# Two attention layers of a graph network: GpSimd's gather program without a loop and without copied indices

## The chip, the cores and the metric

The kernel runs on one core of a Trainium2 chip. A core has five engines that run their own instruction streams side by side and meet at semaphores: TensorE (PE in the profile), VectorE (DVE), ScalarE (ACT), GpSimd (POOL) and SyncE (SP), and 16 DMA engines that move data between the on-chip memory (SBUF) and the chip's main memory. The metric is the device time of one execution in microseconds (us), the median of several runs.

## The reference

Four graph operators stand one behind the other, each followed by a layer normalisation, over 6250 nodes with 64 features and 200000 edges sorted by destination. The change touches the first only, the two attention layers:

```python
def _gat_conv(x, src, dst, W, al, ar, b, act):
    z = (x @ W).reshape(N, H, F)                 # N = 6250, H = 4, F = 64
    el = jnp.sum(z * al, axis=-1)
    er = jnp.sum(z * ar, axis=-1)
    e = jax.nn.leaky_relu(el[src] + er[dst], 0.2)
    m = jax.ops.segment_max(e, dst, num_segments=N)
    ex = jnp.exp(e - m[dst])
    s = jax.ops.segment_sum(ex, dst, num_segments=N)
    alpha = ex / s[dst]
    msg = z[src] * alpha[..., None]
    out = jax.ops.segment_sum(msg, dst, num_segments=N) + b
    return act(out)
...
h = _gat_conv(x, src, dst, W1, al1, ar1, b1, jnp.tanh).mean(axis=-2)
h = _gat_conv(h, src, dst, W2, al2, ar2, b2, lambda v: v).mean(axis=-2)
```

After them come three graph convolutions with edge weights, one plain sum over neighbours and two convolutions with edge features.

## The kernel before

The kernel keeps a table of 6250 rows in main memory (`table_d`: 64 features, a one and four logit parts of each node, 69 floats). In each attention layer the row of every edge's source node is fetched from it. GpSimd does this: `blocks_pool` goes through 98 blocks (`NBLK`) of 2048 edges, each in 16 indirect DMAs (`BK`) of 128 rows, line 826, into one of three ring slots in SBUF (`ring`, `RING` = 3). `gathered[i]` counts what has landed in slot i. Two gathers into the next block stands the store of the finished block to `msg_d` in main memory (`store`, line 800), which waits for all 16 gathers of that block; at the eighth gather GpSimd waits for the store's landing and raises `msg_ready` (`ready`, line 804).

The indices of a gather are a column of `row_idx`. In the loop the block's number is a register, and the gather reads its column not from there but from `idx_cur`, into which a copy on GpSimd (`copy_indices`, line 808) brings four columns at a time (`IDX` = 4), two gathers ahead of their use (`AHEAD_IDX`); the first gather of each four waits for the copy's semaphore `idx_here`. Layer 0's first three blocks are written out, then a loop takes three blocks per turn; layer 1 has its first three blocks written out and then the same loop; the last two blocks of each layer stand behind it. Inside the loop the values that are waited for are computed in registers, and every such wait (`wait_reg`, lines 359 and 360) raises a counter `passed_pool` that nobody reads.

GpSimd is also paced: before every second gather of a block it waits until VectorE's step counter `dve_step` has reached a number that was worked out from the edges (`pace_row`, read into a register on line 812), so that it does not run further ahead of VectorE than intended.

SyncE (`win_sync`) loads for each group of 50 nodes the records (line 505) and, as soon as the block that the group needs is counted in `msg_ready` and the buffer is free, its five windows of messages (`rows_sl<-msg_d`, line 535). VectorE (`win_vector`) does per group: one-hot matrices of edges on adjacency windows (`one_hots`, lines 1051 and 1052; three windows per group in layer 0, two in layer 1), then logits of the messages (`logits`, from line 1074 on, the first instruction that needs them), their maxima (`tops`) and differences. ScalarE and TensorE follow it. There are 125 groups per layer, in 25 rounds of five; a round of VectorE is one turn of its loop. After both attention layers SyncE streams the stored adjacency blocks to TensorE for the six convolutions; GpSimd has nothing to do there. A layer's gathers start from `table_stored`, the landing of its table.

Of the kernel before, what the change touches and what calls it, by code (L numbers as in the profile page):

```python
# [14 lines left out]
I32 = mybir.dt.int32  # L15
# [12 lines left out]
P = 128  # L28
# [55 lines left out]
def build(nc, a):  # L84

    ctx = ExitStack()
    with ctx:
# [37 lines left out]
        def new(parts, *dims):  # L125
            off = top[0]
            top[0] += (int(np.prod(dims)) + 7) // 8 * 8
            return at(off, parts, *dims)
# [25 lines left out]
        xt = new(NT, T, XC)  # L154
        ring = at(xt_off, P, RING, BK * XC)
        row_idx = new(P, EC).bitcast(I32)
        idx_cur = new(P, RING, BK).bitcast(I32)
        er_sb = new(NT, T, H)
        wgat = new(AGG, H, AGG)
        vw = new(F, 2, 2 * H)  # L160
# [146 lines left out]
        def s(name):  # L307
            if name not in S:
                S[name] = sem(name)
            return S[name]  # L310

        for names in (
            "dve_step hi_evacuated prep_step consts_made pool_const  idx_here msg_ready edges_loaded heads_loaded weights_loaded x_loaded rec_stored "
            "ptr_rows_here ptr_back items_out items_back xT_loaded "
            "wgat_loaded el_psum table_made table_stored er_stored "
            "onehot_made rows_weighted adj_psum adj_evacuated seg_evacuated ov_loaded ov_onehot ov_weighted ov_psum ov_added "
            "ov_stored logits_made exp_made win_psum win_evac "
            "ga_loaded ga_top ga_topt ga_diag ga_topp ga_logits ga_exp ga_psum ga_added "
            "ga_stored gat_psum gat_y gat_tanh gat_h gat_hT gat_hTc gat_v gat_xt "
            "gat_done conv_w we_made we_here pn_copied pn_psum pn_evac out_stored ln_var ln_std passed_sp passed_pool "  # L320
            "ov_cleared ov_zeroed ex_loaded ex_again ex_psum ex_done cnt_evacuated low_free top_x top_xt top_xb x_hl x_low cv_self cv_psum cv_aggc cv_y cv_ev cv_yT cv_yTc cv_f cv_done bn_sum bn_mean bn_var bn_std "
        ).split():
            s(names)
# [171 lines left out]
        def win_sync(sp, layer):  # L495
# [24 lines left out]
            for b in rounds_to_last(sp, B):  # L520
                known = {}
                for g in range(NG):
                    if g + AHEAD < NG:
                        known[g + AHEAD] = records(b, g + AHEAD)
                    elif not (isinstance(b, int) and b == B - 1):
                        records(b + 1, g + AHEAD - NG)
                    if g in ER_PART:
                        spread(b, g)
                    offs = known[g] if g in known else offsets(mybir.EngineType.SP, b, g)
                    wait_reg(sp, s("msg_ready"), offs[WG] + layer * NBLK)  # L530
                    done = b * NG + (NGR * layer + g - NG + 1)
                    if not (isinstance(done, int) and done <= 0):
                        wait_reg(sp, s("win_psum"), done)
                    for w in range(WG):
                        sp.dma_start(rows_sl[:, g, w].rearrange("p c x -> p (c x)"), edge_rows(msg_d, offs[w])).then_inc(rows_loaded[g], 16)
# [257 lines left out]
        def blocks_pool(pool, layer):  # L793

            g_ = nc.gpsimd
            uses_before = [layer * len(range(i, NBLK, RING)) for i in range(RING)]

            def store(j, i, uses):
                wait_reg(pool, gathered[i], uses * (16 * BK) + 16 * BK)
                g_.dma_start(msg_d[bass.ds(j * BLK, BLK), :].rearrange("(p k) f -> p (k f)", k=BK), ring[:, i]).then_inc(msg_stored[i], 16)  # L800

            def ready(i, uses):
                wait_reg(pool, msg_stored[i], uses * 16 + 16)
                pool.sem_inc(s("msg_ready"), 1)

            def copy_indices(j, i, k):

                g_.tensor_copy(idx_cur[:, i, k:k + IDX], row_idx[:, bass.ds(j * BK + k, IDX)]).then_inc(s("idx_here"), 1)

            def block(j, i, uses, former, last=False):  # L810
                if not isinstance(j, int) or j >= RING or layer:
                    place = pool.value_load(pace_row[0:1, layer, bass.ds(j, 1)], min_val=1, max_val=HEAD + 2 * NGR * STEPS + PER_BLOCK)
                else:
                    place = None
                for k in range(BK):
                    if place is not None and k % 2 == 0:
                        wait_reg(pool, s("dve_step"), place + k * PER_BLOCK // BK)
                    if k % IDX == IDX - AHEAD_IDX:
                        following = k + AHEAD_IDX
                        if following < BK:  # L820
                            copy_indices(j, i, following)
                        elif not last:
                            copy_indices(j + 1, (i + 1) % RING, 0)
                    if k % IDX == 0:
                        wait_reg(pool, s("idx_here"), j * (BK // IDX) + (layer * NBLK * (BK // IDX) + k // IDX + 1))
                    g_.indirect_dma_start(ring[:, i, k * XC:(k + 1) * XC], None, table_d, bass.IndirectOffsetOnAxis(  # L826
                        ap=idx_cur[:, i, k:k + 1], axis=0)).then_inc(gathered[i], 16)
                    if former is not None and k == BK // 8:
                        store(j - 1, (i - 1) % RING, former)
                    if former is not None and k == BK // 2:  # L830
                        ready((i - 1) % RING, former)

            def former_uses(it, i):
                return it + uses_before[(i - 1) % RING] - (1 if i == 0 else 0)

            copy_indices(0, 0, 0)
            pool.wait_ge(s("table_stored"), 16 * (layer + 1))
            if layer == 0:
                for i in range(RING):
                    block(i, i, 0, None if i == 0 else 0)  # L840
                pool.wait_ge(s("items_back"), 32)
            for it in (rounds(pool, NBLK // RING) if layer else range_from_one(pool, NBLK // RING)):
                for i in range(RING):
                    block(it * RING + i, i, it + uses_before[i], None if first(it) and i == 0 else former_uses(it, i))
            it = NBLK // RING
            for i in range(NBLK % RING):
                block(it * RING + i, i, it + uses_before[i], former_uses(it, i), last=i + 1 == NBLK % RING)
            last = NBLK - 1
            store(last, last % RING, last // RING + uses_before[last % RING])
            ready(last % RING, last // RING + uses_before[last % RING])  # L850

        @block.gpsimd
        def _(pool):
# [1363 lines left out]
```

## Time and profile before

| | us |
|---|---|
| median of 3 runs | 6788.65 |
| lowest and highest run | 6763.08, 6792.3 |
| span of the profiled execution, first to last instruction | 6767.4 |
| VectorE busy in the span | 4197.1 |
| TensorE busy | 4241.0 |
| GpSimd busy | 3514.8 |
| ScalarE busy | 2122.3 |

The profile gives no time of the profiled execution as a whole, only its span; the span is 21.3 us below the median of the runs and 4.3 us above the lowest run. In 40 slices of the span the busy share of each engine can be seen to change three times: at some 170 us (the end of the preparation), at 2.4 ms (the end of the first attention layer) and at 4.8 ms (the end of the second). Shares over the whole span mix stages that have different limits, so each stage is to be read by itself: first what its DVE waits for, then who that in turn waits for.

In the listings "arena" is the one SBUF tensor in which all tiles lie, so a tile is known by the line that uses it. An engine's name with a q behind it (POOLq, SPq, DVEq) is its sequencer, which waits, branches and issues. "issue" as a releaser means that the profile shows nothing for which the engine waited.

### The profile page before, as it was taken

The page shows a single profiled execution, that of the slowest core. Times are in us where ns is not written, and L with a number is a line of the kernel's source. Part 1 is how long each engine was busy: PE and PEld are TensorE (multiplying, and loading weights), DVE is VectorE, ACT ScalarE, POOL GpSimd, SP SyncE. Part 2 cuts the span into 40 slices and gives each one's busy share as a digit, 9 for nine tenths or more (in the row PEclk, how much of TensorE's full clock was granted, in tenths as well). Part 3 has the DMA queues.
Part 4 walks back from the last instruction along what each step waited for, and adds up shares of the span by engine and source line. Part 5 has one row for each costly group of instructions (what it writes and reads, how often), then busy time and mean ns, then how long its engine had stood idle before and what let it go on. Part 6 is the DMA issues. An engine that isn't in the chain of part 4 may idle for free.

```text
span 6767.4 us, 120783 instructions
## 1 busy us (share of the span) xinstructions
PE 4241.0 (63%) x28861; PEld 2819.0 (42%) x28861; DVE 4197.1 (62%) x13512; ACT 2122.3 (31%) x5941; POOL 3514.8 (52%) x4137
## 2 busy tenths in 40 slices
PE   1666666666566674544555555554778888888875
PEld 1333333333333352222322223222567776776764
DVE  4888888888888864777777777777731111224444
ACT  0555555555555532333333333333200000000000
POOL 4788888887777505777887777877000000000000
PEclk9777677777777786666666666666889999999998
DMA  5555555556555523555555555555389898999976
GB/s 96 159 166 161 163 168 157 164 155 172 164 157 166 159 76 90 143 142 135 143 147 141 145 146 143 143 146 141 86 360 416 330 415 335 415 416 400 366 317 274
DMA packets 913170, 1390.70 MB, mean 205 GB/s; under 512 B 481527, under 2 KB 661905, under 8 KB 896598
## 3 DMA queue, kind: packets, MB, share of 16 engines
q1 hardware_dynamic: 576475, 878.02, 37.0%
q0 software_dynamic: 128976, 222.12, 13.8%
q10 hardware_dynamic: 207462, 287.87, 12.3%
q8 instruction: 72, 1.18, 0.1%
q14 instruction: 185, 1.52, 0.1%
HBM read 1014.17 MB, written 373.27 MB: 205 GB/s over the span
## 4 chain that ended last, share of the span: by engine, by line
DVE 36%; DMA 18%; PE 13%; issue 13%; DVEq 11%; POOL 5%; SPq 4%; POOLq 0%; ACT 0%; ACTq 0%
DMA arena<-adj_w_d 9%; DVE arena L1051 7%; POOL arena L826 5%; DMA arena<-adj_c_d 4%; DVEq L1065 3%; DVE arena L1074 3%; DVE arena L1052 3%; PE bank L1842 3%; PE bank L1843 3%; PE bank L1846 3%; DVE arena L1186 2%; DVE arena L1081 2%; DMA arena<-msg_d 2%; DVE arena L1137 2%; DVE arena L1101 2%
## 5 line engine op out<-in xcount | busy, mean ns | idle before, releaser
L826 POOL DMA_INDIRECT arena<-table_d,arena x3136 | 3166.8, 1010 | 1159.3 <-issue 934.6
L1692 PE MATMUL bank<-arena 128*128 128x500 f16 x3750 | 1293.1, 499 | 1486.0 <-DVE arena L1137 1031.1
L1692 PEld LDWEIGHTS bank<-arena 128*128 128x128 f16 x3750 | 436.8, 125 | 2121.3 <-issue 1602.6
L1977 ACT ACTIVATE arena<-arena 128x128 f16<-128x128 f16 x3750 | 1126.1, 398 | 92.0 <-DVEq L1152 81.2
L1842 PE MATMUL bank<-arena 125*128 125x250 f16 x3750 | 862.3, 275 | 173.4 <-DMA arena<-adj_w_d 128.2
L1843 PE MATMUL bank<-arena 125*128 125x250 f16 x3750 | 858.3, 274 | 0.0
L1713 PE MATMUL bank<-arena 128*65 128x40 f32 x7500 | 582.8, 250 | 350.4 <-ACT arena L2020 328.4
L1051 DVE TENSOR_SCALAR arena<-arena 128x500 f16<-128x500 f16 x1875 | 703.6, 375 | 140.6 <-issue 124.6
L1713 PEld LDWEIGHTS bank<-arena 128*65 128x65 f32 x7500 | 567.1, 162 | 453.7 <-ACT arena L2045 436.3
L2045 ACT ACTIVATE arena<-arena 128x600 f32<-128x600 f32 x250 | 175.8, 703 | 1804.2 <-DVEq L1188 1804.2
L1694 PE MATMUL bank<-arena 128*128 128x500 f16 x1875 | 647.0, 464 | 0.0
L1998 ACT ACTIVATE arena<-bank 128x500 f16<-128x500 f32 x625 | 366.8, 587 | 593.4 <-issue 367.6
L1074 DVE TENSOR_TENSOR arena<-arena 128x200 f32<-128x200 f32 x750 | 338.0, 506 | 338.7 <-DMA arena<-msg_d 331.9
L1137 DVE SCALAR_TENSOR_TENSOR arena<-arena,bank 128x250 f16<-128x250 f16 x1250 | 453.6, 411 | 109.4 <-issue 74.8
L1052 DVE TENSOR_SCALAR arena<-arena 128x128 f16<-128x128 f16 x1875 | 520.7, 278 | 0.1
L1846 PE MATMUL bank<-arena 125*128 125x250 f16 x3750 | 443.7, 274 | 109.6 <-DMA arena<-adj_c_d 95.1
L1842 PEld LDWEIGHTS bank<-arena 125*128 125x128 f16 x3750 | 368.1, 98 | 268.8 <-DMA arena<-adj_w_d 154.5
L1846 PEld LDWEIGHTS bank<-arena 125*128 125x128 f16 x3750 | 359.0, 98 | 172.7 <-DMA arena<-adj_c_d 105.5
L1843 PEld LDWEIGHTS bank<-arena 125*128 125x128 f16 x3750 | 364.7, 97 | 51.0
L1694 PEld LDWEIGHTS bank<-arena 128*128 128x128 f16 x1875 | 225.6, 120 | 340.7 <-issue 224.1
L2001 ACT ACTIVATE arena<-bank 128x500 f16<-128x500 f32 x625 | 367.0, 587 | 0.0
L1687 PE MATMUL bank<-arena 128*102 128x30 f32 x1250 | 194.8, 313 | 249.1 <-DVE arena L1137 248.1
(262 smaller groups left out, 4227.7 us busy)
## 6 DMA issues: line engine op xcount, KB each, us to landing
arena<-adj_w_d SPq DMA_DIRECT2D x720, 625.0 KB, 10.6
arena<-adj_c_d SPq DMA_DIRECT2D x345, 625.0 KB, 11.4
adj_w_d<-arena ACTq DMA_DIRECT2D x125, 1250.0 KB
arena<-msg_d SPq DMA_DIRECT2D x1250, 103.5 KB
msg_d<-arena POOLq DMA_DIRECT2D x196, 552.0 KB, 3.3
adj_c_d<-arena ACTq DMA_DIRECT2D x125, 625.0 KB
arena<-table_d,arena POOLq DMA_INDIRECT x3136
arena<-in_edge_features ACTq DMA_DIRECT2D x625, 51.0 KB
```

The source lines that it names most:

```text
L826: g_.indirect_dma_start(ring[:, i, k * XC:(k + 1) * XC], None, table_d, bass.IndirectOffsetOnAxis(ap=idx_cur[:, i, k:k + 1], axis=0)).then ...
L1051: v.tensor_scalar(col_oh[:, slot, c, :], iota_key, key, None, ALU.is_equal)
L1052: v.tensor_scalar(row_oh[:, slot, c, 2, :], iota_lo, rec[:, c * REC + 1:c * REC + 2], None, ALU.is_equal)
L1074: v.tensor_tensor(lg[:, 0:nw, c], bc(rows[:, :, c, F + 1:XC], 3, WN), e, ALU.add)
L1137: last = v.scalar_tensor_tensor(parts[:, h, 1], parts[:, h, 0], -LOW, whole[:, h], ALU.mult, ALU.add)
L1692: mm(wb, lhsT=row_oh[:, slot, c, i, :], rhs=col_oh[:, slot, c, :], start=(c == 0 and i == 0), stop=(c == CH - 1 and i == 1))
L1694: last = mm(cb, lhsT=row_oh[:, slot, c, 2, :], rhs=col_oh[:, slot, c, :], start=(c == 0), stop=(c == CH - 1))
L1713: last = mm(out, lhsT=rows_sl[:, g, w, c, 0:AGG], rhs=grh[:, g, w * CH + c, :], start=(c == 0), stop=(c == CH - 1))
L1842: mm(by_group(out), lhsT=x_one[:, tile, :], rhs=w_slots[slot][0:NT, :, 0, t, :], start=first_, stop=False)
L1843: return mm(by_group(out), lhsT=x_two[:, tile, :], rhs=w_slots[slot][0:NT, :, 1, t, :], start=False, stop=False)
L1846: return mm(by_group(out), lhsT=ones_of(n)[:, t, :], rhs=c_slots[slot][0:NT, :, t, :], start=t == 0, stop=stop)
L1977: last = act_(row_oh[:, slot, c, i, :], row_oh[:, slot, c, 2, :], ACT.Copy, scale=rec[:, c * REC + 2 + i:c * REC + 3 + i])
```

## The change

`blocks_pool` is written without loops. The Python program goes through all 98 blocks of both layers with the block's number as a constant, so that each gather can name its column of `row_idx` directly; `idx_cur`, its copies and the semaphore `idx_here` are gone. The waits for `gathered[i]` and `msg_stored[i]` are on constants and no longer raise `passed_pool`. The paced wait for `dve_step` stays, its value from `pace_row` as before, before every second gather. Gathers, stores and `ready` keep their places. On SyncE the value of the wait for `msg_ready` passes through `& 127`, which leaves it as it is (a block's count is at most 98). The listing of GpSimd's program grows from 500 to 5050 rows.

```diff
--- before.py
+++ after.py
@@ -154,7 +154,6 @@
         xt = new(NT, T, XC)
         ring = at(xt_off, P, RING, BK * XC)
         row_idx = new(P, EC).bitcast(I32)
-        idx_cur = new(P, RING, BK).bitcast(I32)
         er_sb = new(NT, T, H)
         wgat = new(AGG, H, AGG)
         vw = new(F, 2, 2 * H)
@@ -310,7 +309,7 @@
             return S[name]
 
         for names in (
-            "dve_step hi_evacuated prep_step consts_made pool_const  idx_here msg_ready edges_loaded heads_loaded weights_loaded x_loaded rec_stored "
+            "dve_step hi_evacuated prep_step consts_made pool_const msg_ready edges_loaded heads_loaded weights_loaded x_loaded rec_stored "
             "ptr_rows_here ptr_back items_out items_back xT_loaded "
             "wgat_loaded el_psum table_made table_stored er_stored "
             "onehot_made rows_weighted adj_psum adj_evacuated seg_evacuated ov_loaded ov_onehot ov_weighted ov_psum ov_added "
@@ -527,7 +526,7 @@
                     if g in ER_PART:
                         spread(b, g)
                     offs = known[g] if g in known else offsets(mybir.EngineType.SP, b, g)
-                    wait_reg(sp, s("msg_ready"), offs[WG] + layer * NBLK)
+                    wait_reg(sp, s("msg_ready"), (offs[WG] & 127) + layer * NBLK)
                     done = b * NG + (NGR * layer + g - NG + 1)
                     if not (isinstance(done, int) and done <= 0):
                         wait_reg(sp, s("win_psum"), done)
@@ -795,59 +794,37 @@
             g_ = nc.gpsimd
             uses_before = [layer * len(range(i, NBLK, RING)) for i in range(RING)]
 
-            def store(j, i, uses):
-                wait_reg(pool, gathered[i], uses * (16 * BK) + 16 * BK)
-                g_.dma_start(msg_d[bass.ds(j * BLK, BLK), :].rearrange("(p k) f -> p (k f)", k=BK), ring[:, i]).then_inc(msg_stored[i], 16)
-
-            def ready(i, uses):
-                wait_reg(pool, msg_stored[i], uses * 16 + 16)
+            def store(j):
+                i, uses = j % RING, j // RING + uses_before[j % RING]
+                pool.wait_ge(gathered[i], (uses + 1) * (16 * BK))
+                g_.dma_start(msg_d[j * BLK:(j + 1) * BLK, :].rearrange("(p k) f -> p (k f)", k=BK), ring[:, i]).then_inc(msg_stored[i], 16)
+
+            def ready(j):
+                i, uses = j % RING, j // RING + uses_before[j % RING]
+                pool.wait_ge(msg_stored[i], (uses + 1) * 16)
                 pool.sem_inc(s("msg_ready"), 1)
 
-            def copy_indices(j, i, k):
-
-                g_.tensor_copy(idx_cur[:, i, k:k + IDX], row_idx[:, bass.ds(j * BK + k, IDX)]).then_inc(s("idx_here"), 1)
-
-            def block(j, i, uses, former, last=False):
-                if not isinstance(j, int) or j >= RING or layer:
-                    place = pool.value_load(pace_row[0:1, layer, bass.ds(j, 1)], min_val=1, max_val=HEAD + 2 * NGR * STEPS + PER_BLOCK)
-                else:
-                    place = None
+            def block(j):
+                i = j % RING
+                if j >= RING or layer:
+                    place = pool.value_load(pace_row[0:1, layer, j:j + 1], min_val=1, max_val=HEAD + 2 * NGR * STEPS + PER_BLOCK)
                 for k in range(BK):
-                    if place is not None and k % 2 == 0:
+                    if (j >= RING or layer) and k % 2 == 0:
                         wait_reg(pool, s("dve_step"), place + k * PER_BLOCK // BK)
-                    if k % IDX == IDX - AHEAD_IDX:
-                        following = k + AHEAD_IDX
-                        if following < BK:
-                            copy_indices(j, i, following)
-                        elif not last:
-                            copy_indices(j + 1, (i + 1) % RING, 0)
-                    if k % IDX == 0:
-                        wait_reg(pool, s("idx_here"), j * (BK // IDX) + (layer * NBLK * (BK // IDX) + k // IDX + 1))
                     g_.indirect_dma_start(ring[:, i, k * XC:(k + 1) * XC], None, table_d, bass.IndirectOffsetOnAxis(
-                        ap=idx_cur[:, i, k:k + 1], axis=0)).then_inc(gathered[i], 16)
-                    if former is not None and k == BK // 8:
-                        store(j - 1, (i - 1) % RING, former)
-                    if former is not None and k == BK // 2:
-                        ready((i - 1) % RING, former)
-
-            def former_uses(it, i):
-                return it + uses_before[(i - 1) % RING] - (1 if i == 0 else 0)
-
-            copy_indices(0, 0, 0)
+                        ap=row_idx[:, j * BK + k:j * BK + k + 1], axis=0)).then_inc(gathered[i], 16)
+                    if j and k == BK // 8:
+                        store(j - 1)
+                    if j and k == BK // 2:
+                        ready(j - 1)
+
             pool.wait_ge(s("table_stored"), 16 * (layer + 1))
-            if layer == 0:
-                for i in range(RING):
-                    block(i, i, 0, None if i == 0 else 0)
-                pool.wait_ge(s("items_back"), 32)
-            for it in (rounds(pool, NBLK // RING) if layer else range_from_one(pool, NBLK // RING)):
-                for i in range(RING):
-                    block(it * RING + i, i, it + uses_before[i], None if first(it) and i == 0 else former_uses(it, i))
-            it = NBLK // RING
-            for i in range(NBLK % RING):
-                block(it * RING + i, i, it + uses_before[i], former_uses(it, i), last=i + 1 == NBLK % RING)
-            last = NBLK - 1
-            store(last, last % RING, last // RING + uses_before[last % RING])
-            ready(last % RING, last // RING + uses_before[last % RING])
+            for j in range(NBLK):
+                if layer == 0 and j == RING:
+                    pool.wait_ge(s("items_back"), 32)
+                block(j)
+            store(NBLK - 1)
+            ready(NBLK - 1)
 
         @block.gpsimd
         def _(pool):
```

On GpSimd, the start of a block (the third of a loop turn). Before: line 812 reads the pace, 826 is a gather, 808 the copy of four index columns, 800 the store of the former block, 359 computes a value to wait for.

```order
L812 TENSOR_LOAD arena
L812 ISA x2
L359 ISA
L826 DMA arena<-table_d,arena 128x69 x2
L359 REGISTER_ALU
L808 ISA
L808 COPY arena<-arena 128x4
L826 DMA arena<-table_d,arena 128x69
L800 ISA
L800 DMA msg_d<-arena 128x1104
L826 DMA arena<-table_d,arena 128x69
L359 REGISTER_ALU x2
```

After: 810 reads the pace, 814 is a gather, 800 the store, and 358 adds to the value of the paced wait.

```order
L810 TENSOR_LOAD arena
L810 ISA x2
L814 DMA arena<-table_d,arena 128x69 x2
L358 REGISTER_ALU
L814 DMA arena<-table_d,arena 128x69
L800 DMA msg_d<-arena 128x1104
L814 DMA arena<-table_d,arena 128x69
L358 REGISTER_ALU
L814 DMA arena<-table_d,arena 128x69 x2
L358 REGISTER_ALU
```

The copies between gathers are gone, and with them the register work in front of them and in front of the store; two gathers before the store and its place are as they were.

On SyncE, in front of a group's loads of messages. Before: line 514 loads the nodes' logit parts, 535 the messages.

```order
L505 ISA
L505 DMA arena<-rec_d 128x15
L514 DMA arena<-er_d 128x600
L535 ISA
L535 DMA arena<-msg_d 128x207
```

After: the same on lines 513 and 534.

```order
L504 ISA
L504 DMA arena<-rec_d 128x15
L513 DMA arena<-er_d 128x600
L358 REGISTER_ALU
L534 ISA
```

One register instruction stands ahead of the first load of messages and of the wait for `msg_ready` that it carries; nothing else has moved.

## Rows read from the trace of the kernel before

**Rows 1.** Busy time by stage (us; instructions in brackets; clock, DMA share, GB/s).

```profile
core 0: us, PE busy (x) PEld busy (x) DVE busy (x) ACT busy (x) POOL busy (x), PEclk, DMA share, GB/s
200.00:1640.00 1440.00, 889.35 (x5040) 492.04 (x5040) 1182.82 (x3850) 739.38 (x2118) 1161.29 (x1342) 0.72 0.57 163
1640.00:2330.00 690.00, 423.82 (x2425) 230.92 (x2426) 566.32 (x1853) 358.43 (x1031) 528.15 (x625) 0.73 0.57 162
...
2620.00:4753.00 2133.00, 1103.06 (x6346) 613.01 (x6346) 1525.92 (x4860) 806.43 (x2243) 1700.66 (x2018) 0.67 0.53 142
...
4900.00:6767.00 1867.00, 1501.00 (x12998) 1249.23 (x12996) 567.47 (x1876) 99.25 (x240) 0.00 (x0) 0.95 0.90 367
```

**Rows 2.** VectorE's waits in layer 0, 200 to 2425 us: total, times, longest.

```profile
DVE arena L1058 <- issue: 111.2, 117, 4.7
DVE arena L1051 <- issue: 84.1, 305, 0.6
```

**Rows 3.** VectorE's waits in layer 1, 2580 to 4790 us.

```profile
DVE arena L1074 <- DMA arena<-msg_d: 328.3, 51, 14.9
DVE arena L1058 <- issue: 46.6, 115, 0.8
```

**Rows 4.** SyncE's waits in layer 1, 2620 to 4753 us.

```profile
SPq L360 <- POOLq L804: 1152.6, 95, 16.6
```

**Rows 5.** GpSimd's waits in layer 1, 2620 to 4753 us.

```profile
POOL arena L826 <- issue: 314.8, 1053, 0.3
POOL arena L826 <- POOL arena L808: 51.4, 315, 0.2
POOL msg_d L800 <- DMA arena<-table_d,arena: 14.3, 14, 1.6
POOL arena L826 <- DVEq L1065: 14.3, 47, 0.3
POOL arena L826 <- DVEq L1189: 13.0, 53, 0.3
```

**Rows 6.** GpSimd by line, 2580 to 4760 us: busy us, mean ns | idle before.

```profile
L826 POOL DMA_INDIRECT arena<-table_d,arena x1568 | 1577.2, 1006 | 670.3 <-issue 569.7 <-POOL arena L808 52.4 <-DVEq L1065 14.3
L808 POOL COPY arena<-arena 128x4 int32 (+1 forms) x391 | 97.5, 249 | 1.8
L800 POOL DMA_DIRECT2D msg_d<-arena x98 | 58.1, 593 | 18.2 <-DMA arena<-table_d,arena 16.6 <-issue 1.4
```

**Rows 7.** GpSimd in time at layer 1's start, VectorE nearly idle: start, duration, idle before.

```profile
2580.80 0.98 POOL L826 DMA_INDIRECT arena<-table_d,arena  x1 [248.12 <-issue]
...
2583.38 0.97 POOL L826 DMA_INDIRECT arena<-table_d,arena  x1 [0.16 <-POOL arena L808]
2584.65 0.94 POOL L826 DMA_INDIRECT arena<-table_d,arena  x1 [0.30 <-issue]
2585.90 0.95 POOL L826 DMA_INDIRECT arena<-table_d,arena  x1 [0.30 <-issue]
2587.15 0.94 POOL L826 DMA_INDIRECT arena<-table_d,arena  x1 [0.30 <-issue]
2588.09 0.20 POOL L808 COPY arena<-arena 128x4 int32<-128x4 int32 x1
2588.45 0.97 POOL L826 DMA_INDIRECT arena<-table_d,arena  x1 [0.16 <-POOL arena L808]
```

**Rows 8.** GpSimd by line in layer 0, up to 2330 us.

```profile
L826 POOL DMA_INDIRECT arena<-table_d,arena x1568 | 1589.6, 1014 | 489.0 <-issue 364.9 <-POOL arena L808 42.6 <-DVEq L1065 19.8
L808 POOL COPY arena<-arena 128x4 int32 (+1 forms) x392 | 118.2, 302 | 19.4 <-DVEq L900 14.8 <-DVEq L1065 1.7 <-DVEq L1169 1.1
L800 POOL DMA_DIRECT2D msg_d<-arena x98 | 57.8, 590 | 10.0 <-DMA arena<-table_d,arena 8.2 <-issue 1.5
```

**Rows 9.** VectorE by line, 200 to 1640 us, GpSimd at work.

```profile
L1051 DVE TENSOR_SCALAR arena<-arena 128x500 f16<-128x500 f16 x717 | 272.1, 380 | 58.9 <-issue 54.0 <-PE bank L1694 2.4
L1052 DVE TENSOR_SCALAR arena<-arena 128x128 f16<-128x128 f16 x717 | 202.1, 282 | 0.0
```

**Rows 10.** VectorE by line, 2335 to 2425 us, GpSimd idle.

```profile
L1051 DVE TENSOR_SCALAR arena<-arena 128x500 f16<-128x500 f16 x45 | 15.6, 347 | 3.7 <-issue 3.4 <-PE bank L1694 0.2
L1052 DVE TENSOR_SCALAR arena<-arena 128x128 f16<-128x128 f16 x45 | 11.2, 248 | 0.0
```

**Rows 11.** GpSimd's waits in layer 0 from 1640 to 2335 us.

```profile
POOL arena L826 <- DVEq L1189: 13.9, 14, 2.9
POOL arena L826 <- DVEq L1065: 12.5, 18, 3.9
```

**Rows 12.** SyncE's instructions of line 535: duration ns, least, median, greatest.

```profile
L535 SPq FUSED_REGOPS  x615: 37/37/43, 2632.1 to 4749.0; - x154
```

**Rows 13.** GpSimd's loop turn: its branch (first and last start), and in time around it.

```profile
L366 POOLq COMPARE_BRANCH  x1: 58/58/58, 2703.4 to 2703.4; - x1
...
2702.58 0.94 POOL L826 DMA_INDIRECT arena<-table_d,arena  x1 [0.30 <-issue]
2703.82 0.94 POOL L826 DMA_INDIRECT arena<-table_d,arena  x1 [0.30 <-issue]
2705.07 0.94 POOL L826 DMA_INDIRECT arena<-table_d,arena  x1 [0.30 <-issue]
```

## The prediction

> **What bounds the kernel now.** I read first the busy time by stage [rows 1]. GpSimd is busy from 200 to 2330 us (81% of the first window, 77% of the second) and from 2580 to 4753 us (80%), and not at all in the last 1867 us, which are therefore out of reach. VectorE is busy 82% in layer 0 and 72% in layer 1. Neither figure says who waits for whom, so the next views are VectorE's waits, layer by layer.
>
> In layer 0 VectorE never waits for a message: its largest waits have the releaser "issue": 111.2 us ahead of line 1058 (up to 4.7 us, once per turn of its loop) and 84.1 us in small pieces ahead of line 1051 [rows 2]. VectorE sets the pace there; what GpSimd saves in this layer can't shorten it directly. In layer 1 it is the reverse: VectorE waits 328.3 us in 51 places ahead of line 1074, the first instruction on the messages, for their loads from `msg_d` [rows 3]. SyncE, which issues these loads, waits 1152.6 us for line 804, GpSimd's `ready` [rows 4]. And GpSimd waits for nobody: none of its waits ahead of a gather is longer than 0.3 us, also those put down to VectorE's counter, and the stores wait 14 times, 14.3 us in all, for their block's gathers to land [rows 5]. So layer 1 is as long as GpSimd's own stream from 2580.8 us on, and each us taken from that stream is a us of the kernel, until VectorE's 328 us of waiting are used up.
>
> **GpSimd in layer 1, step by step.** Its 2175 us are [rows 6]: 1568 gathers 1577.2, idle before them 670.3 less the 248.1 before the first [rows 7] = 422.2, 391 copies 97.5 and 1.8, 98 stores 58.1 and 18.2. What the change does to each:
>
> - The copies go: 97.5 + 1.8 = 99.3 us.
> - A gather behind a copy has 0.16 us of idle time ahead of it, one behind a gather 0.30 [rows 7]. The 391 gathers behind copies get the longer one: 391 x 0.14 = 54.7 us come back. This is the term that the share of the copies hides; more than half of their time was cover for it.
> - A gather behind a copy takes 0.97 us in the quiet stretch, one behind a gather 0.94 [rows 7]: 391 x 0.03 = 11.7 us go.
>
> That is 99.3 - 54.7 + 11.7 = 56 us, if the gathers stay otherwise as they are. It is the upper end. The lower end comes from the quiet stretch itself: from the gather at 2583.38 to the one at 2588.45 are 5.07 us for four gathers with one copy, against 4 x 1.25 us (2584.65 to 2585.90 to 2587.15) without, so 0.07 us per copy, 391 x 0.07 = 27 us. The ends differ since a copy takes 0.20 us in the quiet stretch and 0.249 on average: it waits for VectorE now and then, and that wait may vanish with it or fall on the gather that now stands there. Gathers wait as well: 1.006 us on average against 0.94 to 0.97. I see no row that decides this and take the middle, 42 us.
>
> The store stays two gathers into the next block, and the block's last gather is now issued less long before it, by the one copy between them, some 0.1 us. For the 14 stores that wait for a landing this is lost again, 1.4 us, and a few more will begin to wait: 2 us against the change. I take 40 us for layer 1.
>
> **VectorE in layer 0.** While GpSimd works the instructions of lines 1051 and 1052 take 380 and 282 ns [rows 9], while it is idle 347 and 248 [rows 10]. So GpSimd's work costs VectorE 33 + 34 ns for each pair; there are three windows of three pairs in each of 125 groups, 1125 pairs, 75 us in the layer. Copies are 118.2 of GpSimd's 1589.6 + 118.2 + 57.8 = 1765.6 busy us [rows 8], 6.7%, so their part by time is 5 us. The bounds are 0 (only gathers disturb) and 12 (a copy disturbs somewhat over twice as much as its share of time). The Trainium skill, GPSIMD Engine Reference, section "Key points", says that GpSimd shares its SBUF interfaces with VectorE and contends with VectorE instructions in a two-port mode or with two SBUF inputs. The rise of lines 1051 and 1052 agrees with it; the page gives no price, so nothing in the sum hangs on it.
>
> Otherwise layer 0 keeps its time. GpSimd gets ahead of VectorE sooner and is then held by the paced wait, as it already is from 1640 us on, where its waits for lines 1189 and 1065 reach 2.9 and 3.9 us [rows 11]. In layer 1 that hold doesn't bite: no wait on the counter is longer than 0.3 us today [rows 5], and VectorE, which raises it, itself comes forward as fast as the messages come.
>
> **The rest costs nothing.** The dropped register work and `passed_pool` lay in GpSimd's sequencer beside gathers of 0.94 us and more. SyncE's added register instruction stands ahead of a wait on which SyncE spends 1152.6 us [rows 4]; one of its register instructions takes 37 ns [rows 12], so even outside that cover it would be 125 x 0.037 = 5 us in layer 1. Behind it are queued only the loads that wait for the same block. What is late next in layer 1 is GpSimd still: 40 us are far less than 328.
>
> **Sum.** 40 + 5 = 45 us. The profiled execution's span of 6767.4 us would become 6722; it lies 21.3 us below the median of the runs, which becomes 6788.65 - 45 = 6743.65, rounded 6744 us.
>
> **Rivals.**
>
> 1. The saving passes to the gathers. If the wait for VectorE moves wholly onto them, layer 1 saves 27 - 2 = 25 us and layer 0 nothing: 6764 us. If their mean rises from 1006 ns to the 1014 ns of layer 0 [rows 8], that is another 1568 x 0.008 = 13 us: 6776 us. For it speaks that GpSimd and VectorE disturb each other; against it that copies are disturbed in proportion more than gathers (0.249 against 0.20, and 1.006 against 0.95 or so), so that fewer disturbed instructions should remain. Chance 0.22, with all savings below 34 us in it.
>
> 2. Slower, by GpSimd's instruction supply. The program grows from 500 to 5050 rows that are each run once. The nearest row for an engine that waits for its own instructions is VectorE's at its loop turn, up to 4.7 us [rows 2]. If GpSimd lost such a time as often as it turned its loop, about once in three blocks, layer 1 would get 33 x 4.7 = 155 us less 40: 6788.65 + 115 = 6904 us. It decides from 40 us on, 1.2 us in three blocks; to be slower by 0.5% (34 us) it takes 2.2 us in three blocks. Against it: the peeled first block of layer 1 is such straight code and runs without a break [rows 7], and VectorE shows the long wait once per turn, not within one. Chance 0.05.
>
> 3. A larger gain. At GpSimd's turn at 2703.4 us gathers follow each other at 0.30 us, as elsewhere [rows 13], so the loop's branches cost nothing that the change could give back. The Trainium skill, Runtime: NRT & Kernel Launch, section "Instruction fetch mechanics", says that a taken branch whose target isn't in the engine's window of instructions stalls for a fetch, and that full unrolling is preferred where possible; here the trace shows no such stall on GpSimd. Were there one of 1 us that the rows hide in longer gathers, layer 1's 31 turns would give 31 us more: 6713 us. Chance 0.07.
>
> 4. That the copies stay, or other instructions move, is excluded by the listing of the two programs: the gathers, the stores and their places are the same.
>
> **How the numbers follow.** The forecast, a gain of 34 to 68 us, has 0.66. A measurement of this kernel can tell about 0.5%, 34 us, from no change; the three runs lie 29 us apart. The upper end of my terms is 56 + 12 = 68 us, 6721; with some 13 us for the runs' scatter the range begins at 6708, which also takes in most of rival 3. Upwards it takes in rival 1's 6764 and part of its rest: 6770. Left out are rival 2, the end of rival 1 and the end of rival 3, about 0.2. Faster by over 0.5%: 0.66 + 0.07 = 0.73, less a little for scatter, 0.72. Within 0.5%: 0.23. Slower: 0.05.
>
> **What would show it.** In layer 1 1568 gathers of 1.00 to 1.01 us with 0.30 us ahead of each, and no copy; GpSimd's stream there takes some 2135 us where it is 2175. VectorE's wait for `msg_d` in layer 1 falls from 328 us to about 290. Layer 0's rounds stay within 0.5 us of their length, and GpSimd begins to be held by the counter well before 1640 us. The last stage is unchanged. The prediction would be wrong if gathers average 1.03 us or more, if idle times of over 0.3 us with releaser "issue" appear ahead of them, or if the stores' wait for landings rises from 14 to 40 us or more.

## The result and the profile after

| | before | after |
|---|---|---|
| median of 4 runs, us | 6788.62 | 6694.61 |
| lowest and highest run | 6763.08, 6792.3 | 6684.06, 6711.46 |
| span of the profiled execution | 6767.4 | 6687.0 |

The ratio is 0.9878 (95% interval 0.985 to 0.9905). The medians lie 94.0 us apart and the two profiled spans 80.4; the ratio, which is estimated from the single runs and not the quotient of the medians, makes it 83 us, with 64 to 102 us in its interval. The forecast was 45 us and at most 80, so the direction was right and the size too small.

GpSimd by line in layer 1, 2570 to 4680 us of the changed kernel; columns as in [rows 6] (busy us, mean ns of one, idle time before, its releasers):

```profile
L814 POOL DMA_INDIRECT arena<-table_d,arena x1568 | 1561.5, 996 | 729.2 <-issue 682.2 <-DMA msg_d<-arena 13.7 <-DVEq L1146 12.8
L800 POOL DMA_DIRECT2D msg_d<-arena x98 | 58.2, 594 | 7.0 <-DMA arena<-table_d,arena 6.5 <-issue 0.2
```

The start of layer 1 on GpSimd in time (start, duration, idle before), as [rows 7]:

```profile
2570.99 0.97 POOL L814 DMA_INDIRECT arena<-table_d,arena  x1 [251.53 <-issue]
2572.26 0.94 POOL L814 DMA_INDIRECT arena<-table_d,arena  x1 [0.31 <-issue]
2573.51 0.94 POOL L814 DMA_INDIRECT arena<-table_d,arena  x1 [0.30 <-issue]
2574.75 0.94 POOL L814 DMA_INDIRECT arena<-table_d,arena  x1 [0.30 <-issue]
```

The copies are gone and every gather has 0.30 us ahead of it, as foreseen. The ledger of GpSimd's stream in layer 1, each number from these rows or [rows 6], the idle time without what stands before the first gather (248.1 and 251.5 us):

| us | before | after | difference |
|---|---|---|---|
| 1568 gathers | 1577.2 | 1561.5 | -15.7 |
| idle before them | 422.2 | 477.7 | +55.5 |
| copies, with idle before them | 99.3 | 0 | -99.3 |
| 98 stores | 58.1 | 58.2 | +0.1 |
| the stores' waits | 18.2 | 7.0 | -11.2 |
| sum | 2175.0 | 2104.4 | -70.6 |

The other 9.8 us lie ahead of it: the first gather of layer 1 starts at 2570.99 us where it was 2580.80. 70.6 + 9.8 = 80.4, the whole difference of the spans; what follows the attention layers is as long as it was.

VectorE's waits in layer 1, 2570 to 4710 us, as [rows 3] (total, times, longest):

```profile
DVE arena L1051 <- DMA arena<-msg_d: 260.1, 45, 11.7
DVE arena L1035 <- issue: 47.1, 117, 0.8
```

It still waits for messages, 260 us where it was 328: GpSimd bounds the layer as before. VectorE by line, 200 to 1640 us of layer 0, as [rows 9]:

```profile
L1028 DVE TENSOR_SCALAR arena<-arena 128x500 f16<-128x500 f16 x727 | 265.0, 365 | 59.7 <-issue 55.7 <-PE bank L1671 1.5
L1029 DVE TENSOR_SCALAR arena<-arena 128x128 f16<-128x128 f16 x727 | 200.1, 275 | 0.0
```

365 and 275 ns where they were 380 and 282.

### The profile page after: what moved, and what is told of

Read it like the earlier page. It is cut to its first block, busy times and chain, and to the rows that moved or that the text cites. A ratio compares the mean times of both kernels' runs of the same rounds, so it can differ in the third digit from the quotient of the medians.

```text
span 6687.0 us, 116651 instructions
## 1 busy us (share of the span) xinstructions
PE 4216.7 (63%) x28861; PEld 2811.6 (42%) x28861; DVE 4179.4 (63%) x13512; ACT 2119.8 (32%) x5941; POOL 3245.1 (49%) x3352
## 4 chain that ended last, share of the span: by engine, by line
DVE 36%; DMA 18%; issue 13%; PE 12%; DVEq 11%; POOL 5%; SPq 4%; ACT 0%; ACTq 0%; POOLq 0%
DMA arena<-adj_w_d 9%; DVE arena L1028 7%; POOL arena L814 5%; DMA arena<-adj_c_d 5%; DVEq L1042 4%; DVE arena L1051 3%; DVE arena L1029 3%; PE bank L1819 3%; PE bank L1820 3%; DVE arena L1058 2%; PE bank L1823 2%; DVE arena L1163 2%; DVE arena L1114 2%; DVE arena L1078 2%; DVE arena L1075 2%
## 5 line engine op out<-in xcount | busy, mean ns | idle before, releaser
L814 POOL DMA_INDIRECT arena<-table_d,arena x3136 | 3113.0, 993 | 1368.4 <-issue 1124.5
L1028 DVE TENSOR_SCALAR arena<-arena 128x500 f16<-128x500 f16 x1875 | 686.4, 366 | 140.6 <-issue 123.9
```

Source lines behind the costliest of these rows:

```text
L1028: v.tensor_scalar(col_oh[:, slot, c, :], iota_key, key, None, ALU.is_equal)
```

## The experiments

The theories: **A**, the copies cost GpSimd's time, and with what they do to gathers and to VectorE they are the gain; **B**, the loop, its register values and the counter `passed_pool` are; **C**, the gathers' wait for the copies' semaphore is. Ratios are to the kernel before, run beside them on the same chip. The kernels e0, e1, e4 and e5 shared one chip, e2, e3, e6 and e7 a second, f1 to f4 a third, h1 to h3 another, k1 to k3 again another.

### The changed kernel again (e0)

No edit.

> The changed kernel once more, as the measure for the others on this chip. Both theories: 80 to 95 us under the kernel before; GpSimd's stream in layer 1 some 2104 us (2175 before), the first gather of layer 1 about 10 us earlier.

Median 6683.72 us against 6783.48: ratio 0.9861 (0.9837 to 0.9884). GpSimd in layer 1:

```profile
L814 POOL DMA_INDIRECT arena<-table_d,arena x1568 | 1560.5, 995 | 730.5 <-issue 685.4 <-DMA msg_d<-arena 14.0 <-DVEq L1146 14.0
L800 POOL DMA_DIRECT2D msg_d<-arena x98 | 58.4, 596 | 6.5 <-DMA arena<-table_d,arena 5.8 <-issue 0.3
```

The ledger repeats within 1 us on each line, while the times of single runs scatter by some 40. How far it repeats from chip to chip is another matter: k1 below runs the same program in layer 1 on another chip, and its stream is 8.7 us shorter. So within one chip a few us in the ledger mean something, and between chips less than 10 us do not. The trace of the kernel before is a single one.

### The copies back, the program still written out (e1)

```diff
+                    if k % IDX == IDX - AHEAD_IDX and ...:
+                        copy_indices(j * BK + k + AHEAD_IDX)
+                    if k % IDX == 0:
+                        pool.wait_ge(s("idx_here"), ...)
...
-                        ap=row_idx[:, j * BK + k:j * BK + k + 1], axis=0)).then_inc(gathered[i], 16)
+                        ap=idx_cur[:, i, k:k + 1], axis=0)).then_inc(gathered[i], 16)
```

> Undoes one part: GpSimd's program stays written out with constants, but the index copies, their semaphore and the gathers from idx_cur are back. Theory A (the copies' own time on GpSimd, with what they do to the gathers and to VectorE, is the gain): like the kernel before, gain 0 to 15 us, copies of about 0.25 us, 0.16 us ahead of the gathers behind them. Theory B (the loop, the register values and passed_pool cost the time, the copies little beside the 0.30 us that stand ahead of each gather anyway): most of the gain stays, 50 to 80 us.

Median 6761.29 us, ratio 0.9978 (0.9963 to 0.9993): 22 us under the kernel before, 78 above the changed one. GpSimd in layer 1:

```profile
L823 POOL DMA_INDIRECT arena<-table_d,arena x1568 | 1578.5, 1007 | 671.0 <-issue 644.6 <-DVEq L1052 11.4 <-DVEq L1176 9.5
L810 POOL COPY arena<-arena 128x4 int32<-128x4 int32 x391 | 97.9, 250 | 1.7
L801 POOL DMA_DIRECT2D msg_d<-arena x98 | 57.9, 591 | 2.5 <-DMA arena<-table_d,arena 2.2
```

Of the changed kernel's 100 us beside the same runs 22 stay (5 to 25 by the ratio's interval), a little more than the 0 to 15 that I expected of theory A and far less than the 50 to 80 of theory B, which falls for the larger part. All lines but one are those of [rows 6] within 2 us; the exception is the stores' wait, 2.5 us where the loop has 18.2. This stream is 2160.7 us (the first gather has 248.9 us of idle time before it), 14.3 shorter than before and 56.3 longer than after. A small part of the gain, some 14 us, thus belongs to the written-out program and came through the stores; it rests on one trace of the kernel before, and e4, written out as well, has the same 2.5 us.

### Copies that nobody reads (e4), and twice as many (e5)

```diff
+                    if k % IDX == 2:
+                        ...
+                        g_.tensor_copy(idx_cur[:, made[0] % RING, 0:IDX], row_idx[:, j * BK:j * BK + IDX]).then_inc(s("idx_here"), 1)
```

In e5 the condition is `k % 2 == 0`. What is left out between the lines is a wait of each copy for the one three copies before it.

> The changed kernel with as many copies of four index columns as before at the same places (392 per layer), but nothing reads them and no gather waits for them; the results are as in the reference. Theory A: 70 to 95 us above the changed kernel, as it is the engine's time that counts. Rival C (it is the gathers' wait for the copy's semaphore that costs): 40 us or less above the changed kernel.

> The same with a copy ahead of every second gather, 784 per layer. Theory A: layer 1 grows by as much again as with 392, about 70 us, and layer 0 by 10 us, so 150 to 175 us above the changed kernel; layer 0 may grow by more where GpSimd no longer keeps ahead of VectorE. Theory B and C: under 80 us above it.

e4: 6759.77 us, ratio 0.9974 (0.996 to 0.9987), 76 us above the changed kernel (e0). e5: 6824.44 us, ratio 1.0071 (1.0048 to 1.0095), 141 above it. GpSimd in layer 1, first of e4, then of e5:

```profile
L822 POOL DMA_INDIRECT arena<-table_d,arena x1568 | 1584.7, 1011 | 668.4 <-issue 640.2 <-DMA msg_d<-arena 11.9 <-DVEq L1051 7.7
L820 POOL COPY arena<-arena 128x4 int32<-128x4 int32 x392 | 100.1, 255 | 1.7
```

```profile
L822 POOL DMA_INDIRECT arena<-table_d,arena x1568 | 1608.5, 1026 | 367.5 <-issue 345.3 <-DVEq L1051 9.3 <-DMA msg_d<-arena 8.3
L820 POOL COPY arena<-arena 128x4 int32<-128x4 int32 x783 | 191.1, 244 | 4.0
L803 POOL DMA_DIRECT2D msg_d<-arena x98 | 57.4, 586 | 2.6 <-DMA arena<-table_d,arena 2.2
```

Theory C falls: copies for which no gather waits cost as much as those of e1. The mean gather rises with the number of copies, 996 (none), 1011 (392), 1026 ns (784), so a copy adds 15 x 1568 / 392 = 60 ns of gather time beside its own 0.25 us and takes back 0.14 us of idle time. Per copy that is 0.25 + 0.06 - 0.14 = 0.17 us, and e5 shows nearly the same price for the second 392, 61 us of stream. My expectation of 150 to 175 us for e5 was a little high: I had 70 us in layer 1 for the second set, and 10 in layer 0, which grows by 1.6 (the first gather of layer 1 comes at 2577.17 us, in e4 at 2575.60).

### One copy per block in the loop (e2, f1, h2, k2)

```diff
-IDX = 4
+IDX = 16
```

> The kernel before with its loop, but one copy of 16 index columns per block in place of four copies of four (IDX = 16; SyncE's value passes through & 127). Theory A: three quarters of the changed kernel's gain, 55 to 70 us under the kernel before. Theory B (loop and registers): 0 to 15 us.

> The kernel with its loop and one copy of 16 columns per block again, since on the second chip layer 1 wasn't bound by GpSimd. On a chip like the first, theory A: from e1 and e4, 392 copies per layer are worth 77 us; a quarter of them stays, so 50 to 60 us under the kernel before, and the loop and the registers have the remaining 20 us of the changed kernel's gain. Theory B: 20 us or less under the kernel before.

> The loop with one copy per block, a third time. On a chip like the first: theory A 2171.9 us less three quarters of 64 us, 2124 us of stream in layer 1, with the stores' wait for landings still at 15 us or more since the loop's registers are still there; theory B over 2150 us.

> As h2: on a chip like the first, theory A gives a stream of 2124 us in layer 1 with 15 us or more of the stores' wait in it, and 45 to 60 us under the kernel before; theory B over 2150 us and under 20 us.

e2, f1 and h2 ran where the kernel takes some 7600 us (below): ratios 0.9985, 1.0005 and 0.9997, each interval with 1 in it, which tells nothing of A and B. k2 ran on a chip like the first: 6724.23 us against 6763.01, ratio 0.9925 (0.9899 to 0.9951). GpSimd in layer 1:

```profile
L826 POOL DMA_INDIRECT arena<-table_d,arena x1568 | 1566.2, 999 | 708.9 <-issue 639.4 <-POOL arena L808 15.8 <-DMA arena<-table_d,arena 14.3
L800 POOL DMA_DIRECT2D msg_d<-arena x98 | 58.8, 600 | 8.9 <-DMA arena<-table_d,arena 4.7 <-issue 3.7
L808 POOL COPY arena<-arena 128x16 int32 (+1 forms) x97 | 25.9, 267 | 0.4
```

With 245.2 us before the first gather the stream is 2123.9 us, as theory A had it. A copy of 16 columns takes 0.267 us, one of four 0.249: what counts is how many copies there are. By the medians the gain is 39 us, under the 45 to 60 expected, and by the ratio 51 (33 to 68), within them. The stores' wait came out at 8.9 us where I had expected 15 or more because the loop is still there; so the loop alone doesn't make 18.2.

### The counter kept (e3)

```diff
-                pool.wait_ge(gathered[i], (uses + 1) * (16 * BK))
+                wait_reg(pool, gathered[i], (uses + 1) * (16 * BK))
```

and the same for `msg_stored`.

> The changed kernel, in which the waits for gathered and msg_stored raise passed_pool again. Theory A: like the changed kernel within 5 us. Theory B: up to 20 us above it.

7595.64 us against 7609.01, ratio 0.9977 (0.9956 to 0.9997), like the other kernels on that chip. It ran there only, and no changed kernel beside it, so the time says nothing of the counter. Its trace does: a store that is held until its block has landed starts 0.61 us or more after the landing, where without the counter it is 0.29 (below). What that adds up to where GpSimd bounds layer 1 wasn't measured.

### The change in layer 1 alone (e6, f2, h1, k1)

```diff
-                blocks_pool(pool, layer)
+                (blocks_pool_in_place if layer else blocks_pool)(pool, layer)
```

> The change in layer 1 alone; layer 0 has the loop and the copies. Theory A: layer 1's stream is some 70 us shorter and layer 0 as before, so 65 to 80 us under the kernel before and about 10 us above the changed kernel. If the gain came from VectorE being disturbed less in both layers, under 50 us.

> The change in layer 1 alone, again. On a chip like the first: 70 to 85 us under the kernel before, the rest of the changed kernel's 95 us in layer 0. On a chip like the second: within 0.3% of the kernel before.

> The change in layer 1 alone, a third time. On a chip like the first: the first gather of layer 1 at 2578 to 2581 us as before the change, GpSimd's stream in layer 1 2101 us as in the changed kernel, so 70 us of the 80 between the two profiles. On a chip like the second: a ratio of 0.995 to 0.998.

> As h1: on a chip like the first, GpSimd's stream in layer 1 is 2101 us, the first gather of layer 1 comes at 2578 to 2581 us, and the time is 60 to 80 us under the kernel before.

On the 7600 us chips the ratios are 0.9977, 0.9959 and 0.997, so the 65 to 80 us expected of e6 didn't come there. k1: 6698.26 us against 6763.01, ratio 0.99 (0.9862 to 0.9938), 65 us. In its trace the first gather of layer 1 in time:

```profile
2579.82 0.97 POOL L874 DMA_INDIRECT arena<-table_d,arena  x1 [251.53 <-issue]
```

and GpSimd by line in that layer:

```profile
L874 POOL DMA_INDIRECT arena<-table_d,arena x1568 | 1555.1, 992 | 729.0 <-issue 682.4 <-DMA msg_d<-arena 15.5 <-DVEq L1206 12.2
L860 POOL DMA_DIRECT2D msg_d<-arena x98 | 58.6, 598 | 4.5 <-DMA arena<-table_d,arena 3.1 <-issue 0.6
```

Layer 0 keeps its old length (2579.8 against 2580.8 us) and layer 1 has the whole of its gain: its stream is 2095.7 us, 79 less than before. That is 9 us more than in the changed kernel, whose program for this layer is the same, and about as much as the changed kernel gains in layer 0 besides. So k1 shows that layer 1 gains without layer 0's change, but not that the two parts add up.

### The store two gathers later (e7, f3, h3, k3)

```diff
-                    if j and k == BK // 8:
+                    if j and k == BK // 4:
```

> The changed kernel with each block's store behind the fifth gather of the next block (k == 4) in place of the third. If the store's wait for its gathers' landing is a cost of its own (7 us in layer 1 of the changed kernel, 18 us before the change), that wait goes to 0 and the kernel gains 5 to 10 us; if the waiting only moves elsewhere, within 5 us of the changed kernel.

> The changed kernel with the store at k == 4, again. On a chip like the first: the store's wait for its gathers' landing (7 us in layer 1) goes, 0 to 10 us under the changed kernel; the ratio to the kernel before 0.985 to 0.986.

> The store at k == 4, a third time. On a chip like the first: the stores' wait falls from 7 to 2 us in layer 1 and the stream from 2101 to 2096 us; no difference that the times can show.

> As h3: on a chip like the first, the stores' wait in layer 1 falls from 7 to 2 us and the stream from 2101 to 2096 us.

On the 7600 us chips the ratios are 0.9973, 0.9969 and 0.9978; the changed kernel has 0.9921 on f3's chip (f4). k3: 6712.38 us, ratio 0.9915 (0.9887 to 0.9944), against the changed kernel's 0.9861. GpSimd's waits in its layer 1:

```profile
POOL arena L814 <- issue: 681.5, 1421, 248.6
POOL arena L814 <- DMA msg_d<-arena: 41.4, 60, 2.8
...
POOL msg_d L800 <- DMA arena<-table_d,arena: 1.9, 1, 1.9
```

The store's wait falls to 1.9 us, but the gather behind `ready` now waits for the store's landing, up to 2.8 us, and the idle time before the gathers is 23 us more than in the changed kernel: its row for line 814 has 749.4 us, 248.6 of them before the first gather. The stream is 2118.3 us, where I had expected 2096. The wait has moved and grown; the place of the change is the better one, by 14 us of stream here and 29 us of time between f3 and f4.

### The changed kernel on another chip (f4)

No edit.

> The changed kernel on the same chip as these three. On a chip like the first a ratio of 0.986; on one like the second, where GpSimd waits for VectorE's counter in both layers, 0.996 to 0.999.

7605.17 us against 7658.81, ratio 0.9921 (0.9894 to 0.9948), a larger gain than I expected there. GpSimd's waits in its layer 1, 3010 to 5500 us:

```profile
POOL arena L814 <- issue: 463.5, 1390, 3.3
POOL arena L814 <- DVEq L1042: 323.2, 87, 10.4
POOL arena L814 <- DVEq L1146: 84.2, 34, 5.3
POOL arena L814 <- DVEq L1166: 43.8, 12, 12.2
```

and the busy times of that stretch, as [rows 1]:

```profile
3010.00:5500.00 2490.00, 1107.02 (x6127) 593.50 (x6126) 1458.85 (x4693) 781.63 (x2167) 1565.65 (x1625) 0.63 0.45 119
```

The instructions take as long as on the first chip, but VectorE is busy only 59% and GpSimd 63% of the stretch. GpSimd is now held by VectorE's counter in layer 1, 451 us in all and up to 12.2 us at a time, where the changed kernel on the first chip has 33 us and never over 0.3. The layer isn't GpSimd's there, and its shorter stream buys less. Why it still buys 0.8% isn't shown.

## Why the prediction was right or wrong

The mechanism was right, the size was not: two terms of layer 1 and the one of layer 0 were too small, and one of them had the wrong sign.

**What bounds each layer**: right. Layer 1 is GpSimd's, as VectorE's remaining 260 us of waits for messages, e4's and e5's price per copy and k1 show; layer 0 is VectorE's. GpSimd is held there earlier than before, as foreseen, up to 4.7 us at a time before 1640 us.

**Copies gone, longer idle time back, gathers behind copies shorter**: the terms 99.3, 54.7 and 11.7 us were right, measured 99.3, 55.5 and 15.7. **The step that failed is the one behind them**: I took 42 us, the middle between 56 and the quiet stretch's 27, because a copy's wait for VectorE might pass to the gather in its place. It did not: in layer 1 a gather behind another gather takes 994 ns on average before and 995 after, and one behind a copy 1021. Measured without the stores the term is 59.5 us in the change and, in e1 against the changed kernel, 61. The gathers' mean fell by 10 ns in the change instead of rising, and e4 and e5 show that it goes up with each set of copies. The quiet stretch was the wrong row for the lower end: it has the copies' floor and not what they cost under load, and layer 1 is nearly all load. That is the rival "the saving passes to the gathers", and the opposite happened.

**The stores' wait**: wrong in sign. I had 2 us against the change; it fell from 18.2 to 7.0 us, 11 for it. Two things are in this number. The one that I had foreseen is there: in the written-out program the stores wait 2.5, 2.5 and 2.6 us with copies (e1, e4, e5) and 7.0, 6.5 and 4.5 without (the changed kernel, e0, k1), since the landing has less time ahead of the store. It costs 2 to 4.5 us, and I had 2. The other, the loop's register work, I had put at nothing: with the same copies the loop has 18.2 us and e1 2.5. What the loop has there can be seen on one late store of the kernel before. The sequencer's wait at line 360 (duration ns, first and last start us):

```profile
L360 POOLq EVENT_SEMAPHORE  x1: 17/17/17, 2735.9 to 2735.9; - x1
```

Its instructions of line 800:

```profile
L800 POOLq FUSED_REGOPS  x1: 46/46/46, 2736.0 to 2736.0; - x1
L800 POOLq MOVE msg_d<-arena x1: 29/29/29, 2736.1 to 2736.1; - x1
```

And the engine in time:

```profile
2736.68 0.58 POOL L800 DMA_DIRECT2D msg_d<-arena  x1 [1.39 <-DMA arena<-table_d,arena]
```

The wait passes at 2735.9, two register instructions follow, and the store starts at 2736.68: over 0.7 us of its 1.39 us of idle time come after the landing. A late store of the changed kernel, in the chain of work that ended last (start us, us, what):

```profile
2803.33 5.28 DMA arena<-table_d,arena
2808.60 0.29 issue
2808.89 0.46 POOL msg_d L800
```

Written out, the store carries its wait itself and has no register instruction ahead: it starts 0.29 us after the landing. So it is at every held store for which the trace has the landing. In layer 1 of the kernel before 14 of them start 0.76 to 0.79 us after it, and the last, whose address is a constant, 0.60; in the changed kernel, e0 and e1 it is 0.29 throughout. Of the 0.47 us between them 0.31 are thus the wait that raises the counter (e3, which keeps it, starts such stores after 0.61 us at the earliest) and the rest goes with the address in registers. I had said that the dropped register work lies beside gathers; it does, except where the sequencer has just been held. An estimate of what it makes: had each of the 20 stores that stand over 0.1 us in layer 1 of the kernel before started 0.47 us sooner (the last 0.31), their wait would be 9.7 us in place of 18.2, 8.5 us less. The other 7 us between the loop and e1 lie in when the gathers land, for which there is one trace of the loop with four copies; k2, which has the loop too, waits 8.9 us. This part stays open.

**VectorE in layer 0**: I had 5 us, bounds 0 to 12. The first gather of layer 1 comes 9.8 us earlier in the change and 12.7 in e0 (2568.07 us), 1.0 in k1, where layer 0 isn't changed. e1 and e4, with copies, have 3.1 and 5.2 us (2577.70 and 2575.60), e5 with twice the copies 3.6 (2577.17), k2 with a quarter of them 7.4 (2573.41) and k3 16.9 (2563.91). VectorE's own busy time says where most of it comes from. Up to 2560 us it has run the same work in each of these traces, some 6420 instructions (columns as in [rows 1]; first before, then after):

```profile
0.00:2560.00 2560.00, 1516.43 (x8735) 870.27 (x8735) 1991.62 (x6419) 1186.45 (x3377) 1782.30 (x2080) 0.75 0.55 151
```

```profile
0.00:2560.00 2560.00, 1515.17 (x8735) 871.11 (x8735) 1978.82 (x6421) 1186.01 (x3377) 1625.61 (x1686) 0.75 0.56 151
```

It falls by 12.8 us, to 1978.1 in e0 and 1978.3 in k3; k1 has 1991.5. It falls only to 1989.7, 1990.6 and 1990.9 in e1, e4 and e5, and in k2 to 1987.6. So some 11 us are the copies' and 1 to 2 the written-out program's. The share of busy time was too small a measure: it gave 5 us. Nor do they grow with the number of copies, since e5 has twice as many and no more of it. Why k3's layer 0 is 7 us shorter than the changed kernel's isn't shown.

**The sum** came out as 45 for 80.4: the missing 35 us are 17.5 in the copies' term (59.5 for 42), 13 at the stores (11 for -2) and 5 in layer 0 (9.8 for 5). The remaining 14 us between the spans' 80.4 and the medians' 94.0 can't be told from scatter: the ratio has 83 us, and the runs of one kernel differ by more than 14. I had carried a gain from one profiled execution over to a median, 21.3 us above its span. The profiles of k1, k2 and k3 show one place where executions differ: from the last gather to the end of the span they take 2029 to 2038 us against the 2015 us of the kernels before and after, in a stage that no kernel here changes.

**The other rivals**: no sign of a want of instructions in the written-out program (no wait ahead of a gather above 0.3 us in layer 1 apart from the first), and none of a stall at the loop's turns: e1, without them, has the gathers' time and idle time of the kernel before within 2 us.

**The effect on the range**: its lower end was made of the upper bounds 56 and 12 us and 13 for scatter. Layer 1's 70.6 us lay above the 56 since the stores were held for a cost. The spans' 80.4 us would just have used up those 81, so the margin for scatter hid the missing term; the median, 6694.61, lies 13 us outside.

## What to carry to other kernels

On an engine that bounds its stage, price a small helper instruction by what stands around it as well: here 0.25 us of copy gave back 0.14 us of the idle time that gathers have anyway, and took 0.06 us more from the gathers beside it. Where rows of a quiet stretch and of a loaded one disagree, the loaded one speaks for a stage under load. And register instructions between a wait and what it releases are free only while the wait has long passed; here they cost up to 0.47 us each time it had not.

## What the runs showed of the hardware

The kernel before takes 6758 to 6799 us on some chips and 7566 to 7684 us on others, but for single runs. On the slow ones the instructions themselves are as long (in f4's layer 1 gathers of 987 ns, lines 1028 and 1029 of 364 and 278), but the idle times between them grow, above all in the attention layers. On VectorE and TensorE most of the growth has no releaser that the profile shows (ahead of VectorE's line 1028 204 us in f4's layer 1, ahead of TensorE's line 1669 568); GpSimd waits for VectorE's counter. GpSimd's streams of the two layers take 2.64 and 2.54 ms in f4, 2.24 and 2.10 ms in the changed kernel's first profile. The changed kernel gains 1.2 to 1.4% on the first kind and 0.8% on one of the second (f4), while e3, which differs from it by the counter alone, gains 0.2% on another, and one copy per block 0.8% on the first (k2) and nothing on the second. What delays the engines there wasn't tried and stays open.
